# Biased logits in SBUF, with all places of the pieces set anew, in a decoder layer on one core

## The chip, the cores and the metric

One core of a Trainium2 chip runs the whole kernel in one launch. The metric is the device time in microseconds. The kernel before took 865.58 us (median of 3 runs, 864.62 to 867.97). The engines are TensorE (PE, its weight loads PEld), VectorE (DVE), ScalarE (ACT), GpSimd (POOL) and SyncE (SP), which issues the transfers.

## The reference

A decoder layer in fp32 on 16 batches of 256 tokens with 256 channels, each of three blocks followed by a layer norm (`_layernorm`):

```python
x = _layernorm(x + _L0_attn_ref(x, ...))       # squared relu of scores, 4 heads, 1024 keys from weights
x = _layernorm(x + _L0_xattn_ref(x, ctx, ...)) # softmax attention, 16 heads of 16 channels
x = _layernorm(x + _L0_ffn_ref(x, ...))        # relu layer of 1024, with one of 8 low-rank experts per token
```

The change is in the second block. For every batch and head it computes

```python
logits = jnp.einsum('bhqd,bhkd->bhqk', Q, K) * scale
D = jnp.clip(frac[:, None, :] - frac[:, :, None], -0.2, 0.2)
bias = ap * jnp.maximum(D, 0.0)[:, None] + an * jnp.minimum(D, 0.0)[:, None]
probs = jax.nn.softmax(gamma * logits + delta * bias, axis=-1)
```

## The kernel before, in words

The 16 batches run through all engines as a pipeline: in one stretch of time the engines work on the scores of batch b+2, the cross attention of batch b, and the feed-forward layer of batch b−2. Each engine has its own program, a walk over a grid (`for g in GRID`) on which every piece of work has a place: `due(g, first, count, step, start, early, late)` yields batch b and unit u where g is `first + step*u + 640*b`; `early` and `late` shift the places of batch 0 and of batch 15. The grid fixes only the order on each engine. Semaphores do the waiting, and an instruction that waits holds up all behind it on its engine. The order of PE's work decides also which of the PSUM banks 0 to 3 a piece gets, since they are handed out in turn (`take`).

Of batch b's 256 x 256 logits for 16 heads, n = 0..15 numbers the heads and p the pairs (n = 2p, 2p+1). The path of a pair is:

- SP, `restack` (L1258): six transfers put the projected queries and keys of four heads into `QS`.
- PE, `logits(p)` (L398 to L407): four matmuls of 48 rows into the two PSUM banks `pL[0]` and `pL[1]` (L405), one per head. Before, they wait for the four minimum pieces of pair p−1 (`s_tt`, 4p).
- POOL, `positive(n)` (L1183): `U[n%2] = alph+ * DP`, 128x512, from SBUF to SBUF. It waits for the minimum pieces of head n−2, which free its buffer.
- DVE, `biased(p)` (L924 to L941): for each of the two heads one addition in place, `L = alph- * DN + L` (L930), with `DN` in SBUF and `L` in PSUM. Then for each head two pieces of 256 columns (L939): `T = -(L + U)`, with the running minimum over the columns into `NM`. `U` and `T` lie in SBUF; there are 2 buffers of `U` and 4 of `T`.
- ACT, `exps(n)` (L711): `P = exp(NM - T)`, two pieces, with the sums.
- PE, `turn(p)` (L421): 16 transposes of 64 rows; ACT copies the result to `STG` (L633, `turned`); PE, `values` (L435) multiplies with the values.

`differences(b)` makes `DP` and `DN` for a batch, by four DVE instructions (L918 twice, L921, L922).

Beside these, DVE has additions of residuals with statistics (`y1` L890, `y2` L963, `y3` L1010, L853, L856), low parts of splits (`cl` L902, `aol` L956, `low` L898, `il` L1001, `projected` L909), normalisations (`centred` L863), the gating of the experts (`gating`, L976 to L989, `g` in L980) and 2 to 3 of the 16 squares per batch (L884). POOL has the other squares (L1165), `gain` (L1158, L1160), `plus` (L1168), `rx` (L1174) and `rsqrt` (L1143 to L1150). ACT has the relus (L655, L763) and the high parts. PE has in addition `scores` (L295), `av` (L308), `otT` (L318), the projections, `op` (L381), `gate`, `gsT`, `uT`, `ffn_in` (L503), `low_rank` (L513) and `ffn_out` (L256). Matmuls of 64 or 48 rows ("half-height") are `scores`, `logits` and `turn`. `filler` runs warm-up matmuls in the head.

Of the kernel before, what the change touches and what calls it, by code (L numbers as in the profile page):

```python
# [5 lines left out]
def decoder_layer(nc, a, out):  # L6
# [13 lines left out]
    with ctx:  # L20
# [225 lines left out]
        def _(eng):  # L246
# [294 lines left out]
            for g in GRID:  # L541
                if g == -2405:
                    pe.wait_ge(s_id, 1)
                    filler(15, pV)
                if g == -1801:
                    pe.wait_ge(s_id, 1)
                    filler(7, pV)
                if g == -2162:
                    pe.wait_ge(s_id, 1)
                    filler(3, pV)  # L550
                if g == 36:
                    pe.wait_ge(s_id, 1)
                    filler(2, pV)
                if g == -605:
                    pe.wait_ge(s_id, 1)
                    filler(6, pV)
                if g == -1468:
                    pe.wait_ge(s_id, 1)
                    filler(3, pV)
                if g == -1217:  # L560
                    pe.wait_ge(s_id, 1)
                    filler(4, pV)
                if g == -428:
                    pe.wait_ge(s_id, 1)
                    filler(16, pV)
                if g == -34:
                    pe.wait_ge(s_id, 1)
                    filler(2, pV)
                if g == -529:
                    pe.wait_ge(s_id, 1)  # L570
                    filler(5, pV)
                if g == 273:
                    pe.wait_ge(s_id, 1)
                    filler(4, pV)
                if g == 196:
                    pe.wait_ge(s_id, 1)
                    filler(8, pV)
                if g == 9946:
# [4 lines left out]
                for b, u in due(g, 1309, 4, 29, early=-19, late=239):  # L583
                    ffn_in(b, u)
                for b, u in due(g, 1310, 4, 29, early=-16, late=370):
                    low_rank(b, u)
                for b, u in due(g, 1426, 8, 24, early=-1, late=2067):
                    ffn_out(b, u)
                for b, _ in due(g, 761, early=-53, late=-6):
# [3 lines left out]
                for b, u in due(g, -943, 4, 148, early=-135, late=-4):  # L593
                    av(b, u)
                for b, u in due(g, 269, 4, 148, early=8, late=49):
# [5 lines left out]
                if g == -884:  # L601
                    bias_o()
                for b, _ in due(g, -276, early=-126, late=40):
                    turned_over("x1T", b, X1, s_x1, 2 * b + 2, s_x1T)
                for b, _ in due(g, -239, early=-877, late=35):
                    kp(b)
                for b, _ in due(g, -223, early=-74, late=52):
                    qp(b)
                for b, _ in due(g, -147, early=182, late=-12):
                    vp(b)  # L610
                for b, _ in due(g, 1118, early=9, late=-31):
                    turned_over("x2T", b, X2, s_x2, 2 * b + 2, s_x2T)
                for b, _ in due(g, 1179, early=-22, late=349):
                    gate(b)
                for b, _ in due(g, 1219, early=18, late=330):
                    gsT(b)
                for b, _ in due(g, 1273, late=351):
                    uT(b)
                for b, u in due(g, -1158, 8, 73, early=-189, late=2):
                    scores(b, u)  # L620
                if g == -2074:
                    xnT(0)
                if g == -807:
                    xnT(1)
                for b, _ in due(g, -1225, start=2, late=-31):
# [3 lines left out]
        def _(eng):  # L629
# [137 lines left out]
            for g in GRID:  # L767
                for b, u in due(g, 1297, 4, 36, early=-7, late=476):
                    ih(b, u)
                for b, _ in due(g, -376, early=903, late=-9):  # L770
# [3 lines left out]
                if g == -4999:  # L774
                    skh(0)
                if g == -1030:
                    skh(1)
                for b, _ in due(g, -1260, start=2, late=-7):
                    skh(b)
                for b, _ in due(g, -491, early=-275, late=2):  # L780
                    heads_out(b)
                for b, u in due(g, 119, 8, 76, early=49, late=33):
                    turned(16 * b + 2 * u)
                    turned(16 * b + 2 * u + 1)
                for b, _ in due(g, 820, early=-13, late=449):
                    aoh(b)
                for b, _ in due(g, 774, early=-64, late=97):
                    rb(b)
                for b, _ in due(g, 977, early=101, late=-53):
                    x2(b)  # L790
                if g == -2658:
                    weight("v", W["v"][0][:, :, :], view(512, 1, 128, 2))
                if g == -1707:
# [630 lines left out]
```

## Time and profile before

| | |
|---|---|
| median of 3 runs | 865.58 us (864.62 to 867.97) |
| the profiled execution | 868.24 us, span 866.4 us, mean granted clock 0.987 |
| busy, PE / PEld | 824.3 / 594.3 us |
| busy, DVE / ACT / POOL | 720.1 / 704.0 / 581.2 us |
| the chain that ended last | PE 84%, DVE 5%, ACT 4%, issue 2%, POOL 2% |
| DMA | 46.32 MB, mean 53 GB/s |

The span is the time from the first to the last instruction of the profiled execution. Busy shares are averages over head, middle and tail, and the head fills a pipeline of several batches, so the middle has to be read by itself. A wait is put down to the instruction that released it. A busy PE is a PE with a matmul in flight, by modelled ends.

### The profile page before, as it was taken

To read this page: it belongs to the slowest core of one execution; us is meant where nothing else is said; L and a number is where in the kernel's file an instruction comes from. 1 tells how busy PE (TensorE), PEld (TensorE's weight loads), DVE (VectorE), ACT (ScalarE), POOL (GpSimd) and SP (SyncE) were. 2 spreads that over 40 slices of the span, in tenths; PEclk is the share of its full clock that TensorE was granted. 3 is DMA by queue.
4 is the path that set the end of the run, shared out by engine and by line. 5 is a ranking of instruction groups with operands and counts; after the bars stand their busy time and mean duration, and the time that the engine had idled before them with its cause. 6 is when DMAs were issued, how large, how long until landed. Compare 5 with 4: busy or idle time off the path is not lost.

```text
span 866.4 us, 23427 instructions
## 1 busy us (share of the span) xinstructions
PE 824.3 (95%) x8444; PEld 594.3 (69%) x8444; DVE 720.1 (83%) x2148; ACT 704.0 (81%) x1930; POOL 581.2 (67%) x754
## 2 busy tenths in 40 slices
PE   7889899999999999999999999999999999999896
PEld 6545556767777676767767676676768667667686
DVE  5887988887888888888888888888888887889854
ACT  3658998897888989798897979888898988888841
POOL 5677878675777868586786768678776867543511
PEclk9998999999999999999999999999999999999899
DMA  7233222222131213223122312313231321323100
GB/s 170 99 65 69 50 56 44 42 40 56 44 62 44 56 38 57 45 52 67 44 57 44 68 26 60 59 45 61 50 63 20 64 55 32 62 45 56 32 14 25
DMA packets 38149, 46.32 MB, mean 53 GB/s; under 512 B 10417, under 2 KB 27313, under 8 KB 38034
## 3 DMA queue, kind: packets, MB, share of 16 engines
q1 hardware_dynamic: 38034, 44.82, 26.0%
q8 instruction: 68, 1.11, 0.6%
q14 instruction: 47, 0.39, 0.1%
HBM read 15.42 MB, written 4.19 MB: 23 GB/s over the span
## 4 chain that ended last, share of the span: by engine, by line
PE 84%; DVE 5%; ACT 4%; issue 2%; POOL 2%; SPq 1%; DMA 1%; POOLq 0%; DVEq 0%; ACTq 0%
PE bank L308 12%; PE bank L503 12%; PE bank L295 11%; PE bank L256 10%; PE bank L421 8%; PE bank L435 7%; PE bank L405 4%; PE bank L381 4%; PE bank L362 2%; PE bank L328 2%; PE bank L342 2%; PE bank L513 2%; PE bank L387 2%; ACT P L711 1%; DVE T L939 1%
## 5 line engine op out<-in xcount | busy, mean ns | idle before, releaser
L1165 POOL TENSOR_TENSOR R<-R 128x512 f32<-128x512 f32 x208 | 220.4, 1063 | 74.8 <-ACT R L655 74.4
L711 ACT ACTIVATE P<-T,NM 128x256 f32<-128x256 f32 x512 | 256.9, 512 | 13.0 <-DVE NM L939 12.9
L1183 POOL TENSOR_SCALAR U<-DP,alph 128x512 f32<-128x512 f32 x256 | 188.1, 736 | 108.5 <-DVE NM L939 72.8
L930 DVE SCALAR_TENSOR_TENSOR bank<-DN,alph,bank 128x512 f32<-128x512 f32 x256 | 180.2, 749 | 47.3 <-PE bank L405 47.1
L939 DVE CUSTOM_DVE_ANT_0 T<-bank,U 128x256 f32<-128x256 f32 x512 | 185.9, 419 | 2.4 <-POOL U L1183 1.3
L655 ACT ACTIVATE R<-bank 128x512 f32<-128x512 f32 x248 | 134.0, 597 | 30.9 <-PE bank L295 29.2
L633 ACT ACTIVATE STG<-bank 128x512 f32<-128x512 f32 x256 | 138.5, 596 | 13.9 <-PE bank L421 12.5
L308 PE MATMUL bank<-R,VS 128*32 128x512 f32 x992 | 120.6, 602 | 6.2 <-DVE R L884 3.8
L295 PE MATMUL bank<-SK,KH 64*128 64x512 f32 x480 | 107.4, 443 | 5.7 <-ACT XO L655 2.4
L711 ACT ACTIVATION_READ_ACCUMULATOR P<-T,NM 128x1 f32 x512 | 103.6, 202 | 0.0
L421 PEld LDWEIGHTS bank<-ident,P 64*128 64x128 f32 x2048 | 77.1, 140 | 36.4 <-issue 27.7
L421 PE MATMUL bank<-ident,P 64*128 64x64 f32 x2048 | 92.2, 229 | 9.5 <-issue 7.3
L295 PEld LDWEIGHTS bank<-SK,KH 64*128 64x128 f32 x480 | 45.8, 185 | 50.3 <-issue 34.1
L503 PE MATMUL bank<-X2H,WIh 128*128 128x256 f32 x256 | 77.9, 304 | 0.0
L256 PE MATMUL bank<-WPh,IH 128*128 128x256 f32 x256 | 76.0, 297 | 0.8 <-DVE IL L1001 0.7
L435 PE MATMUL bank<-STG,VV 128*32 128x256 f32 x1024 | 70.2, 393 | 2.4 <-ACT STG L633 2.4
L503 PE MATMUL bank<-X2L,WIh 128*128 128x256 f32 x256 | 72.1, 281 | 0.0
L503 PE MATMUL bank<-X2H,WIl 128*128 128x256 f32 x256 | 72.0, 281 | 0.0
L256 PE MATMUL bank<-WPl,IH 128*128 128x256 f32 x256 | 71.3, 279 | 0.0
L256 PE MATMUL bank<-WPh,IL 128*128 128x256 f32 x256 | 71.3, 278 | 0.0
L763 ACT ACTIVATE IH<-bank 128x512 fp32r<-128x512 f32 x64 | 37.9, 598 | 39.3 <-PE bank L513 38.9
L1001 DVE SCALAR_TENSOR_TENSOR IL<-bank,IH 128x512 fp32r<-128x512 f32 x64 | 43.7, 689 | 28.8 <-ACT IH L763 28.6
(180 smaller groups left out, 1826.2 us busy)
## 6 DMA issues: line engine op xcount, KB each, us to landing
QS<-QK SPq DMA_DIRECT2D x384, 64.0 KB, 2.3
XG<-in_x SPq DMA_DIRECT2D x16, 256.0 KB, 3.0
CT<-in_ctxT SPq DMA_DIRECT2D x16, 256.0 KB, 2.9
out<-XO SPq DMA_DIRECT2D x15, 256.0 KB, 2.5
FK<-in_frac SPq DMA_DIRECT2D x16, 128.0 KB, 3.2
STG<-in_wiT SPq DMA_DIRECT2D x2, 512.0 KB, 5.5
STG<-in_woT SPq DMA_DIRECT2D x2, 512.0 KB, 4.3
STG<-in_kT SPq DMA_DIRECT2D x2, 256.0 KB, 4.1
```

Of the source, the lines that this page charges most:

```text
L256: i = eng.matmul(o, x, y, start=(first and j == 0), stop=(last and j == 2))
L295: i = eng.matmul(banks[h][:, :], k[half(h), cs], sk(b, part)[half(h), :], start=(j == 0), stop=(j == 2))
L308: m = eng.matmul(pA[o:o + 32, :], VS[:, c, 32 * d:32 * d + 32], rect(16 * b + u), start=(c == 0), stop=(c == 7), skip_group_check=True)
L421: i = eng.transpose(banks[j][:, o:o + 64], P[(2 * p + e) % NP][half(j), q * 256 + k * 128:q * 256 + k * 128 + 128], ident[half(j), half(j)])
L503: eng.matmul(o, w[:, k, cs], x[:, k, :], start=(i + k + j == 0), stop=False, skip_group_check=True)
L633: eng.activation(hi, src, ACT.Copy).then_inc(done, 1)
L655: eng.activation(rect(g), bank_of["sc", b, u][:, :], ACT.Relu).then_inc(s_relu, 1)
L711: eng.activation(P[n % NP][:, cs], T[n % NT][:, cs], ACT.Exp, bias=NM[:, n % 8, q:q + 1], scale=-1.0, accum_out=SU[n // 16 % 2][:, q, seat ...
L930: eng.scalar_tensor_tensor(out=L[:, :], in0=dn[:, :], scalar=alph[:, 16 + h:17 + h], in1=L[:, :], op0=ALU.mult, op1=ALU.add).then_inc(s_t1, 1)
L939: eng.tensor_tensor_reduce(out=t[:, cs], in0=L[:, cs], in1=u[:, cs], scale=-1.0, scalar=BIG, op0=ALU.add, op1=ALU.min, accum_out=NM[:, n % ...
L1165: eng.tensor_tensor(r, r, r, ALU.mult).then_inc(s_sqp, 1)
L1183: eng.tensor_scalar(U[n % NU][:, :], dp[:, :], alph[:, h:h + 1], 0.0, ALU.mult, ALU.add).then_inc(s_u, 1)
```

## The change

The addition writes the `T` buffer in SBUF instead of the PSUM bank, the minimum works in place on `T`, and PE may write the banks again as soon as the two additions are done. The wait for the `T` buffer moves ahead of the addition. `differences` gets one wait more. All places in the grids of the five engines are set anew; `PERIOD`, the buffers, the split of the squares between DVE and POOL and all other pieces stay as they are.

```diff
             def logits(p):
                 G, m = p // 2, p % 2
                 pe.wait_ge(d_q[G % 2], 96 * (G // 2 + 1))
-                pe.wait_ge(s_tt, 4 * p)
+                pe.wait_ge(s_t1, 2 * p)
...
             def differences(b):
                 dve.wait_ge(d_f, 16 * b + 16)
+                dve.wait_ge(d_small, 160)
...
                 for n in pair:
-                    h, L = head(n), pL[n % 2]
-                    eng.scalar_tensor_tensor(out=L[:, :], in0=dn[:, :], scalar=alph[:, 16 + h:17 + h],
+                    h, t, L = head(n), T[n % NT], pL[n % 2]
+                    dve.wait_ge(s_ex, 2 * (n - NT + 1))
+                    eng.scalar_tensor_tensor(out=t[:, :], in0=dn[:, :], scalar=alph[:, 16 + h:17 + h],
                                              in1=L[:, :], op0=ALU.mult, op1=ALU.add).then_inc(s_t1, 1)
                 for n in pair:
-                    u, t, L = U[n % NU], T[n % NT], pL[n % 2]
+                    u, t = U[n % NU], T[n % NT]
                     dve.wait_ge(s_t1, n + 1)
                     dve.wait_ge(s_u, n + 1)
-                    dve.wait_ge(s_ex, 2 * (n - NT + 1))
                     for q in range(2):
                         cs = slice(q * 256, q * 256 + 256)
-                        eng.tensor_tensor_reduce(out=t[:, cs], in0=L[:, cs], in1=u[:, cs], scale=-1.0, scalar=BIG,
+                        eng.tensor_tensor_reduce(out=t[:, cs], in0=t[:, cs], in1=u[:, cs], scale=-1.0, scalar=BIG,
                                                  op0=ALU.add, op1=ALU.min,
                                                  accum_out=NM[:, n % 8, q:q + 1]).then_inc(s_tt, 1)
```

Of the places, those of the pieces around it (the others change in the same manner; the head and the batches 0 and 15 move most):

```diff
 PE
-                for b, u in due(g, -11, 8, 74, early=35, late=5):
+                for b, u in due(g, -11, 8, 75, early=36, late=-1):
                     logits(8 * b + u)
-                for b, u in due(g, 114, 8, 78, early=42, late=7):
+                for b, u in due(g, 120, 8, 78, early=39, late=4):
                     turn(8 * b + u)
-                for b, _ in due(g, -462, early=-136, late=6):
+                for b, _ in due(g, -441, early=-56, late=-1):
                     otT(b)
-                for b, _ in due(g, 856, early=33, late=1):
+                for b, _ in due(g, 884, early=-12, late=-50):
                     op(b)
 ACT
-                for b, u in due(g, 28, 16, 38, early=27, late=6):
+                for b, u in due(g, 29, 16, 38, early=23, late=2):
                     exps(16 * b + u)
 DVE
-                for b, _ in due(g, -71, early=-958, late=113):
+                for b, _ in due(g, -9, early=-966, late=-5):
                     differences(b)
-                for b, u in due(g, 56, 8, 68, early=24, late=5):
+                for b, u in due(g, 15, 8, 78, early=34, late=-3):
                     biased(8 * b + u)
-                for b, u in due(g, 1374, 4, 28, early=7, late=1400):
+                for b, u in due(g, 1341, 4, 21, early=23, late=902):
                     il(b, u)
-                for b, u in due(g, -1121, 16, 40, early=-569, late=-28):
+                for b, u in due(g, -1090, 16, 38, early=-595, late=-31):
                     if on_dve(b, u):
                         square(b, u)
 POOL
-                for b, u in due(g, 23, 16, 38, early=25, late=25):
+                for b, u in due(g, 56, 16, 38, early=23, late=-5):
                     positive(16 * b + u)
-                for b, u in due(g, -1049, 16, 37, early=-214, late=8):
+                for b, u in due(g, -1014, 16, 36, early=-426, late=22):
                     if not on_dve(b, u):
                         square(b, u)
 SP
-                for b, u in due(g, 1005, 4, 116, early=-53, late=209):
+                for b, u in due(g, 720, 4, 86, early=113, late=84):
                     restack(4 * b + u)
-                for b, _ in due(g, 586, start=1, late=256):
+                for b, _ in due(g, 388, start=1, late=91):
                     load_f(b)
-                for b, _ in due(g, -579, start=2, late=-66):
+                for b, _ in due(g, -864, start=2, late=281):
                     load_x(b)
-                for b, _ in due(g, 327, start=1, late=-77):
+                for b, _ in due(g, 86, start=1, late=-329):
                     load_c(b)
```

## Rows read from the trace of the kernel before

**Rows 1.** Busy time by stretch: stretch, then PE, PEld, DVE, ACT, POOL, clock, DMA

```profile
54.00:108.00 54.00, 46.87 (x462) 29.16 (x458) 45.94 (x127) 44.01 (x126) 44.87 (x49) 0.93 0.36 67
447.30:497.30 50.00, 49.54 (x522) 35.54 (x518) 42.93 (x133) 43.48 (x123) 36.41 (x47) 1.00 0.26 52
810.00:866.00 56.00, 44.75 (x430) 37.95 (x426) 32.28 (x100) 23.93 (x64) 12.99 (x22) 0.93 0.07 22
```

**Rows 2.** Line L921, 340 to 600 us and 90 to 760 us: durations, first and last start

```profile
L921 DVE TENSOR_SCALAR DP<-DN x6: 427/428/428, 347.4 to 597.2; 128x512 f32<-128x512 f32 x6
...
L921 DVE TENSOR_SCALAR DP<-DN x14: 426/427/428, 101.3 to 747.3; 128x512 f32<-128x512 f32 x14
```

**Rows 3.** Waits of PE, 297.4 to 597.2 us: us in total, times, longest

```profile
PE bank L421 <- issue: 2.8, 6, 0.5
```

**Rows 4.** Timeline of ACT, 493 to 494.7 us: start, duration, instruction

```profile
493.46 0.20 ACT L711 ACTIVATION_READ_ACCUMULATOR P<-T,NM 128x1 f32 x1
```

**Rows 5.** Timeline of PE, 494.4 to 496 us

```profile
494.55 0.27 PE L421 MATMUL bank<-ident,P 64*128 64x64 f32 x1
```

**Rows 6.** Waits of the whole run: us in total, times, longest

```profile
DVE bank L930 <- PE bank L405: 47.1, 71, 4.1
...
PE bank L405 <- DVE NM L939: 4.2, 6, 1.8
...
PEld bank L405 <- DVE NM L939: 3.2, 4, 2.0
```

**Rows 7.** Groups by line and form: count, busy us, mean ns of one, idle before

```profile
L939 DVE CUSTOM_DVE_ANT_0 T<-bank,U 128x256 f32<-128x256 f32 x512 | 185.9, 419 | 2.4 <-POOL U L1183 1.3 <-issue 0.7
L930 DVE SCALAR_TENSOR_TENSOR bank<-DN,alph,bank 128x512 f32<-128x512 f32 x256 | 180.2, 749 | 47.3 <-PE bank L405 47.1
...
L1001 DVE SCALAR_TENSOR_TENSOR IL<-bank,IH 128x512 fp32r<-128x512 f32 x64 | 43.7, 689 | 28.8 <-ACT IH L763 28.6
...
L902 DVE TENSOR_TENSOR CL<-CT,CH 128x512 fp32r<-128x512 f32 x16 | 15.5, 972 | 0.0
...
L898 DVE TENSOR_TENSOR X2L<-bank,X2H 128x512 fp32r<-128x512 f32 x16 | 10.9, 683 | 0.8 <-ACT X2H L633 0.8
...
L956 DVE TENSOR_TENSOR CL<-AO,CH 128x512 fp32r<-128x512 f32 x16 | 10.6, 664 | 0.7 <-ACT CH L633 0.7
```

**Rows 8.** Single lines: duration ns minimum/median/maximum, first and last start

```profile
L884 DVE TENSOR_TENSOR R<-R x40: 626/680/1532, 15.4 to 752.4; 128x512 f32<-128x512 f32 x40
...
L980 DVE TENSOR_TENSOR g<-g,dec x16: 174/732/745, 143.1 to 849.0; 128x16 f32<-128x16 f32 x16
...
L1183 POOL TENSOR_SCALAR U<-DP,alph x256: 685/695/1197, 62.7 to 821.4; 128x512 f32<-128x512 f32 x128
...
L1165 POOL TENSOR_TENSOR R<-R x208: 1030/1040/1812, 15.4 to 752.5; 128x512 f32<-128x512 f32 x104
```

**Rows 9.** Timeline of DVE, 480 to 491 us: two groups of minima, in part

```profile
480.78 0.42 DVE L939 CUSTOM_DVE_ANT_0 T<-bank,U 128x256 f32<-128x256 f32 x1
...
481.47 0.42 DVE L939 CUSTOM_DVE_ANT_0 T<-bank,U 128x256 f32<-128x256 f32 x1
...
481.81 0.42 DVE L939 CUSTOM_DVE_ANT_0 T<-bank,U 128x256 f32<-128x256 f32 x1
...
488.04 0.42 DVE L939 CUSTOM_DVE_ANT_0 T<-bank,U 128x256 f32<-128x256 f32 x1
```

**Rows 10.** Timeline of POOL, 480 to 491 us

```profile
481.65 0.70 POOL L1183 TENSOR_SCALAR U<-DP,alph 128x512 f32<-128x512 f32 x1 [1.25 <-DVE NM L939]
...
487.65 1.28 POOL L1168 TENSOR_TENSOR X1b<-X,boB 128x512 f32<-128x512 f32 x1
488.91 0.70 POOL L1183 TENSOR_SCALAR U<-DP,alph 128x512 f32<-128x512 f32 x1
489.57 1.05 POOL L1165 TENSOR_TENSOR R<-R 128x512 f32<-128x512 f32 x1
```

More of the change, by code:

```diff
@@ L584, in _ @@
                     ffn_in(b, u)
-                for b, u in due(g, 1310, 4, 29, early=-16, late=370):
+                for b, u in due(g, 1312, 4, 30, early=-18, late=278):
                     low_rank(b, u)
-                for b, u in due(g, 1426, 8, 24, early=-1, late=2067):
+                for b, u in due(g, 1434, 8, 23, early=1, late=1458):
                     ffn_out(b, u)
-                for b, _ in due(g, 761, early=-53, late=-6):
+                for b, _ in due(g, 762, early=-20, late=-25):
@@ L604, in _ @@
                     turned_over("x1T", b, X1, s_x1, 2 * b + 2, s_x1T)
-                for b, _ in due(g, -239, early=-877, late=35):
+                for b, _ in due(g, -232, early=-802, late=31):
                     kp(b)
-                for b, _ in due(g, -223, early=-74, late=52):
+                for b, _ in due(g, -212, early=30, late=11):
                     qp(b)
-                for b, _ in due(g, -147, early=182, late=-12):
+                for b, _ in due(g, -133, early=196, late=-32):
@@ L610, in _ @@
                     vp(b)
-                for b, _ in due(g, 1118, early=9, late=-31):
+                for b, _ in due(g, 1079, early=50, late=24):
                     turned_over("x2T", b, X2, s_x2, 2 * b + 2, s_x2T)
-                for b, _ in due(g, 1179, early=-22, late=349):
+                for b, _ in due(g, 1198, early=-21, late=154):
                     gate(b)
-                for b, _ in due(g, 1219, early=18, late=330):
+                for b, _ in due(g, 1221, early=-3, late=295):
@@ L616, in _ @@
                     gsT(b)
-                for b, _ in due(g, 1273, late=351):
+                for b, _ in due(g, 1276, early=-2, late=290):
                     uT(b)
-                for b, u in due(g, -1158, 8, 73, early=-189, late=2):
+                for b, u in due(g, -1152, 8, 73, early=-164, late=4):
                     scores(b, u)
-                if g == -2074:
+                if g == -4115:
                     xnT(0)
-                if g == -807:
+                if g == -768:
@@ L624, in _ @@
                     xnT(1)
-                for b, _ in due(g, -1225, start=2, late=-31):
+                for b, _ in due(g, -1233, start=2, late=-21):
                     xnT(b)
@@ L775, in _ @@
                     skh(0)
-                if g == -1030:
+                if g == -1460:
                     skh(1)
-                for b, _ in due(g, -1260, start=2, late=-7):
+                for b, _ in due(g, -1252, start=2, late=33):
                     skh(b)
-                for b, _ in due(g, -491, early=-275, late=2):
+                for b, _ in due(g, -494, early=-457, late=14):
                     heads_out(b)
-                for b, u in due(g, 119, 8, 76, early=49, late=33):
+                for b, u in due(g, 121, 8, 75, early=37, late=46):
@@ L783, in _ @@
                     turned(16 * b + 2 * u)
                     turned(16 * b + 2 * u + 1)
-                for b, _ in due(g, 820, early=-13, late=449):
+                for b, _ in due(g, 815, early=-40, late=-71):
                     aoh(b)
-                for b, _ in due(g, 774, early=-64, late=97):
+                for b, _ in due(g, 765, early=-60, late=-27):
                     rb(b)
-                for b, _ in due(g, 977, early=101, late=-53):
+                for b, _ in due(g, 967, early=93, late=83):
@@ L830, in _ @@
                     gs(b)
-                for b, _ in due(g, 1260, early=-27, late=398):
+                for b, _ in due(g, 1264, early=-50, late=278):
                     ulh(b)
-                for b, u in due(g, -1155, 8, 72, early=-433, late=2):
+                for b, u in due(g, -1155, 8, 72, early=-833, late=2):
                     relu(b, 2 * u)
@@ L1118, in _ @@
                     cl(b)
-                for b, _ in due(g, -243, early=-51, late=65):
+                for b, _ in due(g, -225, early=-51, late=11):
                     low("x1T", b, X1L, X1H, s_x1h, s_x1l)
-                for b, _ in due(g, -202, early=-1223, late=33):
+                for b, _ in due(g, -191, early=-1264, late=90):
                     projected("kp", b, 2, 2, s_kh, s_kl)
-                for b, _ in due(g, -179, early=-2, late=35):
+                for b, _ in due(g, -175, early=54, late=85):
@@ L1124, in _ @@
                     projected("qp", b, 1, 0, s_qh, s_ql)
[L1125 removed]
+                for b, _ in due(g, 1197, early=-61, late=75):
                     low("x2T", b, X2L, X2H, s_x2h, s_x2l)
[L1127 removed]
+                for b, _ in due(g, 1201, early=4, late=555):
                     gating(b)
[L1129 removed]
+                for b, _ in due(g, 1274, early=10, late=958):
@@ L1227, in _ @@
                     plus(X1b[b % 2], X1, boB, s_x1b)
-                for b, _ in due(g, 1517, early=-164, late=315):
+                for b, _ in due(g, 1580, early=-201, late=-53):
                     pool.wait_ge(s_x2, 2 * b + 2)
```

207 lines of the change are left out of this document (102 added, 105 removed).

## The prediction

> **What bounds the kernel now.** First the page and a table of stretches [rows 1]. The reader is to see that PE is busy in 49.5 of the 50.0 us of one batch, at the full granted clock, while DVE is busy for 42.9, ACT for 43.5 and POOL for 36.4. The 50.0 us are the distance of one batch from the next: the six `DP` rows between 347.4 and 597.2 us are (597.2 − 347.4) / 5 = 50.0 apart [rows 2]. The waits of the same stretch show one stop of PE per batch, 0.5 us before a turn of P [rows 3]. So in the middle of the run PE sets the pace, and DVE has 50.0 − 42.9 = 7.1 us of idle time per batch in reserve. Head and tail are looser (PE 46.9 of 54 and 44.8 of 56 us). The profiled execution took 868.24 us around a span of 866.4; that is 2.7 us above the median of the runs, 865.58, and I take 2.7 off at the end.
>
> How much lateness the chain can take is the third thing to read. The running minimum (L939) feeds the exponentials (L711), and these feed PE's turn (L421), which PE reaches in a fixed order. For turn 6 of the batch shown, the last exponential ended at 493.46 + 0.20 = 493.66 and PE began at 494.55: 0.9 us to spare [rows 4, 5]. Over the eight turns of a batch this slack runs from 0.9 to 3.7 us.
>
> **The change part by part.**
>
> *Bank freed earlier.* `logits(p)` now waits for the two additions of pair p−1, not for its four minimum pieces. PE stood for `NM` 4.2 us and its weight loads 3.2 us in the whole run, partly the same stops [rows 6], and none of that in the steady stretch [rows 3]. Gain between 0 and 7.4 us; I take 4. DVE's 47.1 us of waiting for logits [rows 6] isn't a wait for the bank: PE merely comes to them late in its order, and that order is almost the same after the change (in the middle of the run two neighbouring swaps, turn 1 with `otT` and `op` with one `ffn_out`; no half-height group is joined or split by them).
>
> *Cheaper instructions.* The addition (L930) writes SBUF instead of PSUM. Its row is 749 ns; the same operation with PSUM and SBUF in and SBUF out (L1001) is 689 [rows 7]. That is 60 ns × 16 = 1.0 us of DVE per batch. The minimum (L939, 419 ns) now has no PSUM input. A `tensor_tensor` of 512 columns costs 683 ns with one PSUM input (L898) and 664 with two SBUF inputs when little runs beside it (L956) [rows 7]: some 20 to 25 ns × 32 = 0.8 us. Together 1.8 us per batch, so DVE's need is 42.9 − 1.8 = 41.1. The Trainium skill ("VectorE: DVE Perf Modes", the errata section) gives a fixed part of 120 cycles for a PSUM source and 58 for SBUF, by which the minima would save an estimated 65 ns × 32 = 2.1 us; the rows show a third of that, and the sum goes by the rows.
>
> *Two SBUF inputs beside POOL.* This is the term that decides. Today each minimum reads one PSUM and one SBUF tensor and takes 419 ns whatever POOL does. After the change it reads `T` and `U`, both in SBUF. The trace has DVE instructions of that kind, and they are slow when POOL works [rows 7, 8]: `CL<-CT,CH` takes 972 ns on the mean where its twin `CL<-AO,CH`, which falls in quiet moments, takes 664; the squares on DVE have a minimum of 626 and a maximum of 1532; the tiny `g<-g,dec` of 16 columns has a minimum of 174 and a median of 732. The longest are about one POOL instruction longer than the shortest (a square on POOL takes 1040, a `U` 695 [rows 8]), and POOL's own have long outliers too (1812 and 1197). So the two engines take turns. The Trainium skill ("SBUF — State Buffer", Who interferes with whom) says the same: a Vector instruction with two SBUF inputs and a GpSimd one that reads SBUF exclude each other for the whole instruction. The trace agrees with it (174 against 732 ns).
>
> Per pair there are four minima in 1.4 us. I lay POOL's rows beside two such groups [rows 9, 10]. In the one at 480.78, POOL asks at 481.65, gets in behind the third minimum and holds the fourth up: +0.6 us. In the one at 488.04, POOL has been on `X1b` since 487.65 (to 488.93), then has a `U` and a square ready: 0.9 + 0.7 + 1.0 and a last piece of 0.5 = +3.1 us. The six other groups of this batch, laid out in the same way, give 3.3, 0.6, 2.9, 0.1, 0.6 and 2.5; all eight 13.8 us. If the batch gets longer, POOL is less dense: 13.8 × 50 / 55.5 = 12.4. The bounds: below, nothing (the custom instruction doesn't collide); above, each of the 32 minima waits for one whole POOL instruction of 0.87 us on the mean, 28 us. I take 12.4, since the queue of POOL is the one traced.
>
> **The sum.** DVE needs 41.1 + 12.4 = 53.5 us per batch, plus idle time that dependences leave. Of the 7.1 us now idle most is waiting for PE or ACT, which goes when DVE is the late one; I keep 2.0. A batch then takes 55.5 us, 5.5 more. Between the first `DP` with full load (101 us) and the last (747 us) lie 13 distances [rows 2]: 13 × 5.5 = 71.5. In the head and the last batches fewer squares run; the pairs there pay perhaps 0.6 us each, of which most lies beside other waits: +3. The earlier bank: −4. 868.2 + 71.5 + 3 − 4 = 938.7, and less 2.7 it is **936**.
>
> *What costs nothing.* The addition now waits for the exponentials of the same `T` buffer, earlier by two additions (1.4 us). Nothing in the list of waits shows DVE held by them, and they end several us before. If they became late, the whole DVE queue would stand behind that wait: squares, `y1`, `projected`. The wait for small loads in `differences` is already passed. The new places change PE's steady order hardly at all. On DVE they spread the eight pairs (step 78 for 68), on POOL they shift squares and rsqrt by one or two neighbours, on SP the restacking of a batch is bunched (steps of 86 for 116) and its loads of x, c and f follow it. SP issues are short and nothing waited for them in the steady stretch. Head: the loads of c and v, the squares and the warm-up matmuls change order. Head and tail together hold PE idle time of 7.1 + 11.2 us [rows 1] plus the first 54 us, so new places can win perhaps 8 us and lose as much; I take 0.
>
> **The rivals.**
>
> *A, faster: no collision of the custom instruction.* All rows that collide are ordinary ones; L939 has its own program, and no row has it with two SBUF inputs. Then DVE has 1.8 us more slack, PE's 0.5 us stop per batch goes (13 × 0.5 = 6.5) and 4 us of bank waits: 865.6 − 10.5 = 855, between 850 and 861. The same time comes if POOL's pieces fall between the minima. Against it: two streams from SBUF are what the slow rows have in common. Chance 0.17.
>
> *B, no change: the collisions fit into the reserve.* DVE has 7.1 + 1.8 = 8.9 us per batch. If the collisions cost less than that and no group of minima is later than the slack of its turn, the time stays at 862 to 869. Against it: four of eight groups get 2.5 us or more and turn slacks begin at 0.9. The point of decision is 8.9 us per batch. Chance 0.13.
>
> *C, my forecast, slower:* DVE takes PE's place; own range 900 to 980. Chance 0.60.
>
> *D, still slower: strict alternation.* Each minimum frees POOL, POOL's next instruction gets in before the next minimum. 25 of 28 us would make 41.1 + 25 + 2 = 68 us per batch and some 1100 us. Against it: the `U` instructions are released only by the minima themselves (two `U` buffers), so POOL has mostly one or two ready. Chance 0.04. The rest, 0.06, is a smaller slowdown of 870 to 900, where half the collisions find slack.
>
> **The numbers.** About 0.5% (4.3 us) is what a measurement of this kernel can tell from no change. Slower takes C, D and the rest, 0.70; same is B, 0.13; faster is A, 0.17. The range leaves out D, the upper end of C and the lower half of A: 857 to 980.
>
> **What would show it.** Right: rows of the minimum with a mean of 0.65 to 0.85 us instead of 0.42, and a long maximum near 1.4; the addition at 0.69; some `U` rows and squares longer too; PE's share falling from 99% to about 90% in the middle with PE waiting for ACT's P; `DP` rows 55 us apart; granted clock still mostly full. Wrong: minima at 0.39 to 0.42 whatever POOL does (A), or long minima with `DP` rows still 50.0 apart (B).

## The result, and the profile after

The changed kernel takes 922.16 us (median of 4 runs, 919.86 to 923.62) where the kernel before took 865.32 in the same comparison: a ratio of 1.0648, with a 95% interval of 1.0614 to 1.0683. The forecast was 936 in a range of 857 to 980; the direction and the collisions held, but two sizes that went into the sum were off in opposite directions, and the way by which PE is held up was another. One run of a later kernel took 1112 us at a granted clock of 0.652 and is left out; all other runs are alike.

First the busy time of three stretches: stretch, PE, PEld, DVE, ACT, POOL, granted clock, DMA. It answers to [rows 1].

```profile
54.00:108.00 54.00, 42.90 (x449) 27.22 (x450) 49.25 (x121) 40.77 (x118) 45.46 (x48) 0.97 0.34 61
496.50:550.70 54.20, 50.20 (x521) 35.89 (x520) 48.43 (x133) 43.78 (x120) 39.91 (x48) 1.00 0.24 47
866.00:921.80 55.80, 43.68 (x415) 36.97 (x414) 32.11 (x100) 23.69 (x64) 15.37 (x22) 0.93 0.05 15
```

One batch now takes 54.2 us instead of 50.0. DVE works 48.4 of them, 5.5 more than the 42.9 of before, and POOL 3.5 more. PE, which had 0.5 us of gaps, has 4.0. Head and tail hardly changed in length: the `DP` row at 101 us stands where it stood. The `DP` rows, one per batch, say the same (they answer to [rows 2]; the two rows are of 340 to 660 us and of 90 to 810 us):

```profile
L922 DVE TENSOR_SCALAR DP<-DN x6: 426/427/428, 369.5 to 640.3; 128x512 f32<-128x512 f32 x6
...
L922 DVE TENSOR_SCALAR DP<-DN x14: 426/427/429, 101.2 to 800.7; 128x512 f32<-128x512 f32 x14
```

The same 13 distances took 747.3 − 101.3 = 646.0 us before and take 699.5 now. These 53.5 us are nearly the whole difference of 56.8.

The groups by line show what became longer (they answer to [rows 7]):

```profile
L940 DVE CUSTOM_DVE_ANT_0 T<-T,U 128x256 f32<-128x256 f32 x512 | 257.9, 558 | 2.5 <-POOL U L1184 2.5
...
L1184 POOL TENSOR_SCALAR U<-DP,alph 128x512 f32<-128x512 f32 x256 | 223.9, 878 | 170.8 <-DVE NM L940 123.8 <-DVE DP L922 47.0
L932 DVE SCALAR_TENSOR_TENSOR T<-DN,alph,bank 128x512 f32<-128x512 f32 x256 | 178.9, 740 | 35.0 <-PE bank L405 32.8
```

The minimum went from 419 to 558 ns on the mean. The line's own answer (minimum/median/maximum) shows that this is not a general slowing: 95 of the 512 take more than 500 ns, the others at most 448. Before, the longest was 425 ns. Before and after:

```profile
L939 DVE CUSTOM_DVE_ANT_0 T<-bank,U x512: 408/419/425, 63.5 to 825.4; 128x256 f32<-128x256 f32 x171
...
L940 DVE CUSTOM_DVE_ANT_0 T<-T,U x512: 409/421/1500, 60.0 to 879.1; 128x256 f32<-128x256 f32 x171
```

Where they are long, POOL is at work. This is the worst of the eight groups of minima of a batch, in the timeline of DVE (start, duration, instruction), and then POOL's timeline of the same microseconds:

```profile
525.90 1.05 DVE L940 CUSTOM_DVE_ANT_0 T<-T,U 128x256 f32<-128x256 f32 x1
...
526.89 1.49 DVE L940 CUSTOM_DVE_ANT_0 T<-T,U 128x256 f32<-128x256 f32 x1
...
528.32 1.50 DVE L940 CUSTOM_DVE_ANT_0 T<-T,U 128x256 f32<-128x256 f32 x1
...
529.75 0.41 DVE L940 CUSTOM_DVE_ANT_0 T<-T,U 128x256 f32<-128x256 f32 x1
```

```profile
524.65 2.03 POOL L1166 TENSOR_TENSOR R<-R 128x512 f32<-128x512 f32 x2
526.64 1.46 POOL L1159 TENSOR_TENSOR XN<-XN,gB 128x512 f32<-128x512 f32 x1
528.18 1.35 POOL L1161 TENSOR_TENSOR XN<-XN,bB 128x512 f32<-128x512 f32 x1
```

The two engines take turns. A minimum issued at 525.90 ends at 526.95, 0.3 us after POOL's second square; the next waits out the whole multiplication `XN<-XN,gB`, the third the whole addition `XN<-XN,bB`, and only the fourth finds POOL idle. The group takes 4.3 us; four undisturbed minima take 1.5. All 95 long minima of the run overlap a 128x512 instruction of POOL that reads SBUF; none is long beside POOL's 128x2 instructions (76 minima, at most 426 ns).

Last, PE's waits between 306 and 631 us, six batches (they answer to [rows 3], where there was one line):

```profile
PE bank L485 <- DVE U L990: 8.3, 6, 1.4
PE bank L421 <- DVE X2L L898: 5.5, 6, 0.9
PE bank L447 <- DVE IL L1002: 3.5, 5, 0.7
PE bank L421 <- issue: 2.8, 6, 0.5
PE bank L362 <- DVE X1L L898: 1.6, 6, 0.3
PE bank L295 <- ACT STG L633: 1.2, 5, 0.2
```

Here a reader sees how collisions on DVE reach PE. In these six batches PE doesn't wait for the minima, nor for the exponentials that need them, as the prediction had it (`PE <- ACT P` isn't in the list); it waits for pieces that stand behind them in DVE's queue. The largest is `U2` of the gating (L990), which follows the group shown above; then the low parts of x2 and x1, and `IL`. The sum is 22.9 us, 3.8 per batch, against 0.5 before.

### The profile page after: what moved, and what is told of

It reads as the page before. It is cut to its first block, busy times and chain, and to the rows that moved or that the text cites. A ratio compares the mean times of both kernels' runs of the same rounds, so it can differ in the third digit from the quotient of the medians.

```text
span 921.8 us, 23525 instructions
## 1 busy us (share of the span) xinstructions
PE 835.8 (91%) x8444; PEld 602.3 (65%) x8444; DVE 803.6 (87%) x2148; ACT 707.9 (77%) x1930; POOL 636.0 (69%) x754
## 4 chain that ended last, share of the span: by engine, by line
PE 43%; DVE 34%; issue 10%; POOL 6%; ACT 5%; SPq 0%; DMA 0%; DVEq 0%; POOLq 0%; ACTq 0%
DVE T L940 14%; PE bank L256 8%; PE bank L503 6%; PE bank L295 5%; PE bank L421 4%; PE bank L308 4%; DVE T L932 4%; PE bank L435 3%; POOL R L1166 2%; DVE XN L863 2%; PE bank L405 2%; PE bank L362 2%; ACT P L711 2%; PE bank L381 2%; POOL U L1184 2%
## 5 line engine op out<-in xcount | busy, mean ns | idle before, releaser
L1184 POOL TENSOR_SCALAR U<-DP,alph 128x512 f32<-128x512 f32 x256 | 223.9, 878 | 170.8 <-DVE NM L940 123.8
L940 DVE CUSTOM_DVE_ANT_0 T<-T,U 128x256 f32<-128x256 f32 x512 | 257.9, 558 | 2.5 <-POOL U L1184 2.5
L1166 POOL TENSOR_TENSOR R<-R 128x512 f32<-128x512 f32 x208 | 226.4, 1091 | 35.8 <-ACT R L655 35.1
L932 DVE SCALAR_TENSOR_TENSOR T<-DN,alph,bank 128x512 f32<-128x512 f32 x256 | 178.9, 740 | 35.0 <-PE bank L405 32.8
L711 ACT ACTIVATION_READ_ACCUMULATOR P<-T,NM 128x1 f32 x512 | 101.5, 198 | 0.0
L295 PEld LDWEIGHTS bank<-SK,KH 64*128 64x128 f32 x480 | 47.0, 185 | 51.7 <-issue 32.7
L503 PE MATMUL bank<-X2H,WIh 128*128 128x256 f32 x256 | 80.3, 314 | 0.0
L503 PE MATMUL bank<-X2L,WIh 128*128 128x256 f32 x256 | 74.3, 290 | 0.0
L503 PE MATMUL bank<-X2H,WIl 128*128 128x256 f32 x256 | 74.2, 290 | 0.0
L405 PE MATMUL bank<-QS 48*128 48x256 f32 x512 | 63.0, 314 | 4.6 <-DMA QS<-QK 2.6
```

The costliest lines, as they stand in the source:

```text
L295: i = eng.matmul(banks[h][:, :], k[half(h), cs], sk(b, part)[half(h), :], start=(j == 0), stop=(j == 2))
L503: eng.matmul(o, w[:, k, cs], x[:, k, :], start=(i + k + j == 0), stop=False, skip_group_check=True)
L711: eng.activation(P[n % NP][:, cs], T[n % NT][:, cs], ACT.Exp, bias=NM[:, n % 8, q:q + 1], scale=-1.0, accum_out=SU[n // 16 % 2][:, q, seat ...
L932: eng.scalar_tensor_tensor(out=t[:, :], in0=dn[:, :], scalar=alph[:, 16 + h:17 + h], in1=L[:, :], op0=ALU.mult, op1=ALU.add).then_inc(s_t1, 1)
L940: eng.tensor_tensor_reduce(out=t[:, cs], in0=t[:, cs], in1=u[:, cs], scale=-1.0, scalar=BIG, op0=ALU.add, op1=ALU.min, accum_out=NM[:, n % ...
L1166: eng.tensor_tensor(r, r, r, ALU.mult).then_inc(s_sqp, 1)
```

## The experiments

Two theories were to be told apart. **Theory 1** puts the time to the minima with two SBUF inputs, which exclude POOL's reading instructions. **Theory 2** puts it to the new places. The medians of the kernel before were 866.9 to 867.6 us in these series, and each cost below is against that of its own series. In cuts of code `...` stands for what is left out.

**New code at the old places, and the new places with the old code.** The first kernel takes `biased` and the wait in `logits` from the changed kernel and every place from the one before:

```diff
-                pe.wait_ge(s_tt, 4 * p)
+                pe.wait_ge(s_t1, 2 * p)
...
-                    eng.scalar_tensor_tensor(out=L[:, :], in0=dn[:, :], scalar=alph[:, 16 + h:17 + h],
...
+                    eng.scalar_tensor_tensor(out=t[:, :], in0=dn[:, :], scalar=alph[:, 16 + h:17 + h],
...
-                        eng.tensor_tensor_reduce(out=t[:, cs], in0=L[:, cs], in1=u[:, cs], scale=-1.0, scalar=BIG,
+                        eng.tensor_tensor_reduce(out=t[:, cs], in0=t[:, cs], in1=u[:, cs], scale=-1.0, scalar=BIG,
```

> The new code (addition into T, minimum from T and U, banks freed after the additions) with all places as before. Theory 1, collisions of two-input SBUF minima with POOL: the slowdown is all here, 905 to 935 us, minima with a mean of 0.53 us or more and a maximum near 1.5, groups of four minima beside squares 2 to 4 us long. Theory 2, the new places cost the time: 860 to 870 us, though single minima may be long.

Measured: 914.06 us, ratio 1.0552 (1.0528 to 1.0576). The minima are 409/418/1515 ns, 565 on the mean. The second kernel is the changed one with these lines turned back.

> The new places with the old code (addition in place in PSUM, minimum from PSUM and U, banks freed by the minima). Theory 1: 860 to 875 us, minima at 0.42 us with no spread. Theory 2: 905 to 925 us. If both parts cost something, 875 to 900.

Measured: 879.43 us, ratio 1.0148 (1.0119 to 1.0177), with all minima between 410 and 427 ns. So both parts cost: the code 46.5 us, the places 11.9. The two add up to 58.4, against 56.8 for the whole change. Theory 1 carries four fifths of it.

**Only POOL's writing.** If the minima wait for POOL because it reads SBUF, a POOL that only writes shouldn't hold them up. The new code at the old places, first with `U` filled by a memset:

```diff
-                eng.tensor_scalar(U[n % NU][:, :], dp[:, :], alph[:, h:h + 1], 0.0, ALU.mult,
-                                  ALU.add).then_inc(s_u, 1)
+                eng.memset(U[n % NU][:, :], 0.0).then_inc(s_u, 1)
```

> The new code at the old places, but POOL fills U by a memset, which reads nothing; this leaves out the product of the positive differences with alpha. If only POOL instructions that read SBUF collide with the minima, the part of U goes and that of the squares and sums stays: 885 to 910 us, minima beside U rows at 0.42 us, beside squares still up to 1.5 us. If a writing POOL instruction collides too, the time stays within 5 us of the new code at old places. Theory 2: 860 to 870 us like that one.

Measured: 899.3 us, ratio 1.0383 (1.0357 to 1.0408), 15 us less than with the product; the mean of the minima went from 565 to 524 ns. Then with POOL's squares as memsets too, and the control, the kernel before with the same two memsets:

```diff
-                eng.tensor_tensor(r, r, r, ALU.mult).then_inc(s_sqp, 1)
+                eng.memset(r, 0.0).then_inc(s_sqp, 1)
```

> New code at old places, with POOL's U and POOL's squares both replaced by memsets, which write and read nothing; this leaves out the product for the positive part of the bias and POOL's squares. What POOL still reads are gain, sums and rx. If whole POOL instructions that read SBUF are what the minima wait for, their mean falls to 0.42 to 0.45 us and the time is within 8 us of the control with the same memsets in the kernel before. If writes collide as well, or the new code is slow for another reason, it stays 25 us or more above the control.

> Control: the kernel before with POOL's U and squares as memsets (the same parts left out). PE sets the pace in the kernel before, so a lighter POOL should change little: 858 to 868 us.

Measured: 862.78 us (ratio 0.9954, 0.9932 to 0.9976) and 856.78 us (0.9880, 0.9857 to 0.9904). The control came out 1 us below its expected range. The new code costs 6 us more than its control, where it cost 46 with POOL reading. The mean of the minima is 462 ns, just above the 0.42 to 0.45 us that were expected, since POOL's remaining sums still meet 26 of them. In the middle of the run these cost next to nothing, for a batch takes 50.1 us against 50.0 in the control:

```profile
L921 DVE TENSOR_SCALAR DP<-DN x6: 427/427/428, 386.9 to 637.6; 128x512 f32<-128x512 f32 x6
...
L921 DVE TENSOR_SCALAR DP<-DN x6: 427/428/428, 382.8 to 632.7; 128x512 f32<-128x512 f32 x6
```

Of the 4.7 us by which the two profiled executions differ, 4 lie in the first four batches; what makes them there isn't shown. In the new code with memsets, DVE and then POOL around two groups of minima:

```profile
483.01 1.32 DVE L939 CUSTOM_DVE_ANT_0 T<-T,U 128x256 f32<-128x256 f32 x1
...
490.90 0.42 DVE L939 CUSTOM_DVE_ANT_0 T<-T,U 128x256 f32<-128x256 f32 x1
...
491.25 0.42 DVE L939 CUSTOM_DVE_ANT_0 T<-T,U 128x256 f32<-128x256 f32 x1
```

```profile
482.76 1.28 POOL L1160 TENSOR_TENSOR XN<-XN,bB 128x512 f32<-128x512 f32 x1
...
491.04 0.53 POOL L1183 MEMSET U<- 128x512 f32 x1 [1.25 <-DVE NM L939]
491.51 0.53 POOL L1165 MEMSET R<- 128x512 f32 x1
```

The minimum at 483.01 waits for the addition that began at 482.76; those at 490.90 and 491.25 run through a memset as if it were not there. A memset is also shorter than a square (534 against 1040 ns), so the times of these runs alone don't separate fewer readers from a lighter POOL; the single rows do. In this kernel 202 minima overlap a memset and no 128x512 reader, and take 411 to 426 ns; the 26 long ones all overlap a 128x512 reader.

**Half the dose.** At the old places only the odd head of each pair goes by SBUF, and the banks are freed by the minima:

```diff
+                    if n % 2:
+                        dve.wait_ge(s_ex, 2 * (n - NT + 1))
+                    eng.scalar_tensor_tensor(out=(t if n % 2 else L)[:, :], in0=dn[:, :],
...
+                        eng.tensor_tensor_reduce(out=t[:, cs], in0=(t if n % 2 else L)[:, cs], in1=u[:, cs],
```

> Old places; only the odd head of each pair is added into T and has its minima from SBUF, the even head stays in PSUM; banks are freed by the minima as before. Half as many minima can collide. If DVE's idle 7.1 us per batch took collisions up, half the dose would cost nothing: 863 to 870 us. If single late pieces stop PE wherever they fall, it costs about half of the full dose: 880 to 900 us.

Measured: 897.23 us, ratio 1.0355 (1.0326 to 1.0384), 64% of the cost of the full dose. Its groups show both kinds side by side in one kernel:

```profile
L942 DVE CUSTOM_DVE_ANT_0 T<-T,U 128x256 f32<-128x256 f32 x256 | 138.1, 576 | 0.7 <-POOL U L1186 0.7
...
L942 DVE CUSTOM_DVE_ANT_0 T<-bank,U 128x256 f32<-128x256 f32 x256 | 97.5, 418 | 1.3 <-POOL U L1186 1.3
```

and its busy time for one batch:

```profile
481.50:533.20 51.70, 49.68 (x520) 35.62 (x519) 45.58 (x133) 43.44 (x122) 38.76 (x48) 1.00 0.25 50
```

DVE is idle for 51.7 − 45.6 = 6.1 us of this batch, and yet the batch takes 1.7 us more than the 50.0 of before. The time is in the range that was expected for late pieces that stop PE. But the late pieces are here the minima themselves: this kernel keeps the late release of the banks, and nearly the whole loss is PE standing in front of the logits for the minima of the pair before:

```profile
PE bank L405 <- DVE NM L942: 9.4, 6, 1.6
```

So the idle time of DVE isn't a reserve for this delay, since it lies at other places than the handover. It can be one where the delays are small: with the memsets above, some 1.4 us of collisions per batch (32 minima, 43 ns longer on the mean) went by at 50.1 us.

**The early release of the banks.** The changed kernel with the old wait in `logits`:

```diff
-                pe.wait_ge(s_t1, 2 * p)
+                pe.wait_ge(s_tt, 4 * p)
```

> The changed kernel, but the logits wait for the minima of the pair before, as they used to. If the early release is worth something once the minima are long, this is slower than the 922 us of the changed kernel: 924 to 935 us. If PE comes late to the logits anyway: 920 to 924 us.

Measured: 936.45 us, ratio to the kernel before 1.0799 (1.0740 to 1.0858). This is 1 us above the upper expectation. In the changed kernel the release is worth 14 us. With the old wait PE stands in front of the logits for the minima, up to 2.3 us at once. But its stops in six batches aren't longer in sum (22.1 us against 22.9); they lie elsewhere. What grew is the time in which PE is busy, from 50.2 to 51.8 us per batch, at a lower granted clock. Waits with the old wait, then five batches of the changed kernel and five with the old wait:

```profile
PE bank L405 <- DVE NM L940: 13.6, 6, 2.3
...
369.50:640.30 270.80, 250.78 (x2592) 179.21 (x2594) 242.03 (x661) 218.90 (x601) 199.39 (x235) 1.00 0.25 48
...
373.20:651.10 277.90, 259.22 (x2594) 181.11 (x2589) 236.41 (x661) 218.57 (x600) 199.77 (x235) 0.96 0.24 46
```

The release is a repair of a damage that the change itself does: where most minima are short, as in the two kernels with memsets, the new code with the release is not faster than the old one without.

**Which places cost.** The kernel before with the new places of one engine at a time:

```diff
 DVE (first kernel)
-                for b, u in due(g, 56, 8, 68, early=24, late=5):
+                for b, u in due(g, 15, 8, 78, early=34, late=-3):
                     biased(8 * b + u)
...
 POOL (second kernel)
-                for b, u in due(g, -1049, 16, 37, early=-214, late=8):
+                for b, u in due(g, -1014, 16, 36, early=-426, late=22):
...
```

> The kernel before with the new places of DVE alone. All new places together cost some 12 us. If the late pieces of DVE do it (the split of x2 stands behind a normalisation that takes turns with POOL, and PE waits for it), DVE's places alone cost 5 to 12 us: 871 to 880 us, with PE waiting for DVE X2L. If it is the orders of the engines against each other, less than 3 us: 863 to 869 us.

> The kernel before with the new places of POOL alone. If POOL's order matters by what runs beside the normalisations and splits of DVE, XN, XO and CL rows change and the time is 868 to 878 us. If POOL's idle 13 us per batch covers it: 863 to 869 us.

Measured: 920.58 us for DVE's places (ratio 1.0622, 1.0580 to 1.0665) and 872.23 us for POOL's (1.0074, 1.0049 to 1.0099). The second lies in the first range of its expectation. The first was a miss of both expectations. DVE's new places among the other engines' old ones cost 54 us, although all engines' new places together cost 12. The trace shows a stop at a place that neither parent has: PE's scores wait 1.8 us in each batch for the bank that `y1` on DVE (L890) frees.

```profile
PE bank L295 <- DVE XG L890: 10.6, 6, 1.8
PE bank L421 <- DVE X2L L898: 3.7, 6, 0.6
```

This stop doesn't account for all of it. Two neighbouring batches of this kernel have the same stops of PE (1.8 + 0.6 + 0.5 us), and the second takes 1.4 us more. In it, PE's granted clock is at the lower of its two levels (1.2 GHz, 0.50 in the row) for 3.4 us from 496.6 us on, just after PE stood 1.75 us for `XG`; single matmuls of L381 take 0.41 us there, and 0.28 in stretches at the full clock:

```profile
421.70:474.30 52.60, 49.73 (x522) 35.66 (x518) 43.56 (x133) 43.56 (x121) 36.94 (x47) 1.00 0.25 50
474.30:528.30 54.00, 51.17 (x522) 37.01 (x518) 43.38 (x133) 43.64 (x121) 36.98 (x47) 0.97 0.24 48
...
498.00:500.00 2.00, 2.00 (x11) 2.00 (x11) 2.00 (x7) 1.32 (x5) 1.83 (x3) 0.50 0.00 0
```

By the mean clocks (0.969 of 919.8 us, 0.987 of 866.4) this kernel is at the lower level for some 57 us and the kernel before for 23. With `U` as a memset, too, batches with such a stretch take 53.4 us and those without 52.0. At 1.4 us per 3.4, an estimate is that 14 of the 54 us are the clock's. In the same way some 10 of the 14 us of the old wait above, and 4 of the 57 us of the whole change, are an estimate of the clock's part.

The places of the five engines are one schedule, and a part of it can't be judged alone. The stop for `X2L` is in the kernel with all new places as well (3.7 us in six batches there too): part of what the new places cost. POOL's places cost 5 us. The waits show one new stop of PE of 0.2 us per batch; DVE's squares went from 799 to 891 ns on the mean and `XN` from 758 to 936, while `XO` stayed at 443. How the rest comes about isn't shown.

**Mending one stop.** In the new code at the old places PE's largest stop was 1.5 us per batch before the turn of `U2` (L485). Here this turn stands one piece later on PE, and ACT's copy of it with it:

```diff
-                for b, _ in due(g, 1273, late=351):
+                for b, _ in due(g, 1274, late=350):
                     uT(b)
-                for b, _ in due(g, 1260, early=-27, late=398):
+                for b, _ in due(g, 1270, early=-37, late=388):
                     ulh(b)
```

> New code at old places, with PE's turn of U2 one piece later, behind the last scores, and ACT's copy of it behind the relu. In the new code at old places PE waited 1.5 us per batch at this turn for the gating on DVE, which stands behind the most delayed minima. If each stop is a matter of its own, 12 us come back: 897 to 905 us. If PE just meets the late DVE at the next piece, 910 to 920 us.

Measured: 914.38 us (median of 3 runs), ratio 1.0550 (1.0528 to 1.0573), the same as without it. PE now stops 1.5 us in front of the scores instead, and still for DVE's L989. The scores get the PSUM bank that held the gating's input, and L989 is also what frees this bank. So the late piece stops PE at the next place that depends on it:

```profile
PE bank L295 <- DVE U L989: 8.7, 6, 1.5
```

**Half-height groups joined on PE.** Two attempts to better the kernel before by its order alone. In the first, the scores of units 4, 5 and 6 move behind the full-height work and stand next to logits or turn; their relus move behind it.

```diff
                 for b, u in due(g, -1158, 8, 73, early=-189, late=2):
-                    scores(b, u)
+                    if u not in [4, 5, 6]:
+                        scores(b, u)
+                for b, _ in due(g, -855, early=-200, late=2):
+                    scores(b, 4)
...
```

> The kernel before, with three of the eight groups of scores moved past the full-height work between them and the next logits or turn, so that half-height work stands together three times more per batch (and the relus that follow are placed behind). If each switch between full and half height costs the 0.1 us that the first matmul of a group shows, six switches per batch save 0.6 us: 855 to 861 us. If later scores and relus hold up squares and so minima, that is lost: 866 to 880 us.

Measured: 925.48 us, ratio 1.0687 (1.0647 to 1.0726), far above both expectations. PE now stops before a turn for the bank of the gating, which DVE frees (9.3 us in six batches), and 8.8 us (2.8 before) in front of turns without a releaser that the profile shows. In the second only the scores of unit 2 and turn 1 move, each past one piece:

```diff
-                    turn(8 * b + u)
+                    if u != 1:
+                        turn(8 * b + u)
+                for b, _ in due(g, 195, early=39, late=4):
+                    turn(8 * b + 1)
...
-                    scores(b, u)
+                    if u not in [2]:
+                        scores(b, u)
+                for b, _ in due(g, -1011, early=-190, late=2):
+                    scores(b, 2)
```

> The kernel before with two small moves on PE: the scores of unit 2 behind values, next to turn 2, and turn 1 behind one ffn_out, next to scores 1, so that two groups of half-height matmuls join others. If a switch between heights costs 0.1 us, four fewer per batch save 0.4 us: 858 to 862 us. If the old order was tight, 866 to 880 us.

Measured: 883.81 us, ratio 1.0194 (1.0165 to 1.0222), 4 us above the upper expectation. PE stops twice as often before turns, and before scores for ACT's copies out of the banks:

```profile
PE bank L421 <- issue: 7.2, 12, 0.7
PE bank L295 <- ACT STG L639: 4.7, 6, 0.8
```

Whatever a switch between heights costs, the 0.4 us that four fewer could save are outweighed by waits (a batch takes 51.4 us). Scores next to a turn ask for four banks in a row, and I read the waits as those for the copies that free them; that wasn't tested further. No version here that computes the whole layer beats the kernel before.

## Why the prediction was right, and where its sizes were off

**The bound.** PE was the bound, with 7.1 us of DVE's time idle; that reading held. So did these signs: a longest minimum near 1.4 us (1.50), `DP` rows some 55 us apart (54.2), PE's share near 90% (50.2 of 54.2, 93%). Three didn't: the mean of the minima is 0.56 us and not 0.65 to 0.85, the addition takes 0.74 and not 0.69, and PE doesn't wait for ACT's P in the middle of the run. The steps were these.

**Bank freed earlier (forecast −4).** In its direction right for the kernel with long minima, where the release is worth 14 us, but as a gain over the kernel before it wasn't there. The 7.4 us of PE waits for `NM` lay in head and tail, and the kernel with memsets and the release is 6 us slower than its control without.

**Cheaper instructions (forecast 1.8 us per batch).** Wrong by an order of magnitude. The addition into SBUF costs 740 ns instead of 749, not 689, and an undisturbed minimum 421 or 418 instead of 419. Only 16 × 9 ns = 0.15 us per batch came. The row that I took as a twin (L1001) is the same kind of instruction, but with an immediate scalar where the addition reads one per partition, and with its PSUM input first instead of second. Which of these makes the other 50 ns wasn't tried. The saving that the figures of the Trainium skill ("VectorE: DVE Perf Modes", the errata section) would give for the minima, an estimated 65 ns each, isn't there at all: the measured rows have 419 with a PSUM input and 418 to 421 without.

**The collisions (forecast 12.4 us per batch).** The mechanism was right; the size was less than half. In the batch shown the eight groups of minima take 1.5, 2.1, 1.5, 1.5, 4.3, 2.6, 1.5 and 1.5 us: 4.6 us more than eight undisturbed ones. DVE's busy time grew by 5.5 us; 1.2 of these also come with the new places alone. The failing step is the line "since the queue of POOL is the one traced". (The eight terms of the forecast add up to 13.7 and not 13.8, which changes nothing.) I had moved the traced POOL rows along, but POOL isn't a fixed background. The new code at the old places has the same group as the one at 488.04 in the forecast, with `X1b` before it. In DVE's timeline, then POOL's:

```profile
517.69 1.20 DVE L939 CUSTOM_DVE_ANT_0 T<-T,U 128x256 f32<-128x256 f32 x1
...
519.51 0.41 DVE L939 CUSTOM_DVE_ANT_0 T<-T,U 128x256 f32<-128x256 f32 x1
```

```profile
517.32 1.29 POOL L1168 TENSOR_TENSOR X1b<-X,boB 128x512 f32<-128x512 f32 x1
519.34 1.07 POOL L1183 TENSOR_SCALAR U<-DP,alph 128x512 f32<-128x512 f32 x1 [0.73 <-DVE NM L939]
```

The forecast had `X1b`, `U` and the square each hold up one minimum, +3.1 us. Only `X1b` does, +0.8. The next `U` is released by minima that are themselves late, so POOL stands still for 0.73 us; and when it starts, beside minima that follow each other without a gap, it is `U` that becomes longer (1.07 us instead of 0.70) and not the fourth minimum. The same holds for a `U` released in the middle of a group, for which the forecast had +0.6 us: at 510.43 us of the same trace the group has four minima of 0.42 us and a `U` of 1.06. Rival D (strict alternation throughout) is rare: all four minima are long in 2 of the 128 groups of the changed kernel, three in a row in another 13.

**What idle time remains (forecast 2.0).** It is 54.2 − 48.4 = 5.8 us. I took DVE for the new bound, with hardly a gap, and it isn't the bound. Neither engine is full: PE stops for single late pieces of DVE (3.8 us per batch), then is late itself, and DVE waits for its logits and projections. That this loop sets the pace is read from the waits; that a stop moves to the next place when it is taken away is shown by the experiment with the turn of `U2`. This error and the one before pulled in opposite directions, so that 55.5 us per batch was forecast and 54.2 came; that the two nearly cancel is luck. With the measured sizes of the additions and collisions and the forecast's own 2.0 us of idle time, the same sum gives 42.9 + 5.5 + 2.0 = 50.4 us, nearly no change. 53.5 us over the 13 batches are the result.

**The new places (forecast 0 ± 8).** They cost 12 us. I had looked at PE's order, found it almost unchanged in the middle of the run, and concluded from that. The order of DVE mattered: the normalisation `XO` now runs beside POOL (788 ns at the median instead of 407), and `X2L` stands behind `XN` and stops PE by 0.6 us a batch. The kernel before, then the one with new places and old code:

```profile
L863 DVE TENSOR_SCALAR XO<-X2b,SMd x30: 394/407/1117, 195.4 to 847.4; 128x256 f32<-128x256 f32 x30
...
L863 DVE TENSOR_SCALAR XO<-X2b,SMd x30: 404/788/1120, 203.4 to 857.9; 128x256 f32<-128x256 f32 x30
```

So a single-input instruction from SBUF to SBUF, too, can take turns with POOL. How much of the 12 us each of the two makes wasn't tried.

**The rivals.** A (the custom instruction doesn't collide) fell at once: 1500 ns. B (the reserve takes it up) fell with the result, and with half the dose: 6.1 us idle and still 30 us slower. It is what happens only with the few collisions that are left beside memsets.

## What to carry to other kernels

Before moving an operand of a DVE instruction from PSUM to SBUF, count its SBUF inputs, and look what POOL reads at that time; a PSUM operand may be what keeps the two engines apart. Idle time of an engine is a reserve only at the point where it lies: when another engine takes the results in a fixed order, the slack of each single handover counts, and not only of the one looked at: the turns had 0.9 us or more, but PE came to stop at the gating and at low parts of splits. A stop can also cost more than its length, when PE's clock falls behind it. When estimating a contention from an old trace, let the other engine's queue react, for part of it is released by the very instructions that become late.

## What the runs showed of the hardware

A custom DVE instruction with two SBUF inputs waits out whole 128x512 POOL instructions that read SBUF (409 ns at the least, up to 1515 in the new code at old places), and isn't touched by POOL memsets (0.42 us beside them). The rule of the Trainium skill ("SBUF — State Buffer", Who interferes with whom), that only GpSimd instructions that read count against a two-input one, is borne out by these rows. The single-input normalisations do wait for memsets: in the kernel before with memsets two of them in a row take 0.80 and 0.76 us beside memsets, where the shortest takes 0.40.

```profile
125.58 1.48 DVE L863 TENSOR_SCALAR XN<-XG,SMa 128x256 f32<-128x256 f32 x2
```

```profile
125.70 0.54 POOL L1183 MEMSET U<- 128x512 f32 x1
126.39 1.14 POOL L1165 MEMSET R<- 128x512 f32 x2 [0.15 <-ACT R L655]
```

A stretch of 3.4 us at 1.2 GHz cost 1.4 us, by two neighbouring batches with the same stops of PE. Not expected was that neither the addition's output in SBUF nor the minimum's SBUF input made the undisturbed instruction noticeably shorter (740 against 749, 418 against 419 ns).
